# Two orders in the attention loop: a projection piece one group earlier on TensorE, and the copies of finished sums one group up on VectorE

## The chip, the cores and the metric

The kernel runs on one core of one Trainium2 chip. The metric is the device time of one execution in microseconds (us). Of three runs of the kernel before, the median is 2519.34 us (2516.67 to 2519.8). The engines are TensorE (PE, and PEld for its weight loads), VectorE (DVE), ScalarE (ACT), GpSimd (POOL) and SyncE (SP). Each engine takes its instructions strictly in the order in which the program lists them.

## The reference

Eight sequences of 1024 tokens with 512 features pass a causal attention of 16 heads (32 features each), a residual and a layer norm, then a layer of eight experts of which each token takes the best one, a residual and a layer norm. All is float32.

```python
Q, K, V = x @ W_Q.T, x @ W_K.T, x @ W_V.T           # split in 16 heads
attn  = einsum('bhqd,bhkd->bhqk', Q, K) * scale      # causal mask
y     = einsum('bhqk,bhkd->bhqd', softmax(attn), V)
x     = layernorm(x + y @ W_O.T)
probs = softmax(x @ router_w.T + router_b)
x     = layernorm(x + (x @ expert_w[top1].T + expert_b[top1]) * max(probs))
```

## The kernel before

`attend` handles the eight sequences (batches) one after the other. A batch has four units (`u` = 0 to 3) of four heads. The work of a unit is a chain through the engines:

- **projections**: Q and K of a unit are four tiles `("p", u, i)` of 12 matmuls each (L975), made in three pieces of four matmuls, two units ahead. ScalarE rounds the finished tile to its high part (`high`, L646) and VectorE subtracts it to get the low part (`low`, L750). Only then is the PSUM bank free (`proj_free`), and the next tile's first piece can start in it. DMAs of SP and POOL (L443) put the parts into the stacks.
- **maxima**: before a unit's scores are exponentiated, the row maxima of all its scores are needed. 38 maximum tiles (L1032) are computed one unit ahead and reduced on VectorE (`reduce_tile`, L789 or, with the causal mask, L794). Three PSUM banks take turns (`max_ring`), so maximum tile i waits until VectorE has reduced tile i-3.
- **scores**: 12 groups (`j` = 0 to 11, called first to twelfth here) of four tiles (L1044), each followed by an Exp on ScalarE (L704). Two banks take turns in units 0 and 1, more in units 2 and 3.
- **weighing**: two groups later (`LAG` = 2) `weigh` (L1064) multiplies the probabilities with V into `y_ps` and with ones into `den_ps`, 8 instructions of four column tiles. A unit's sums run over groups 1 to 4 (first half of the queries) and 5 to 12 (second half). At the end of a half VectorE copies `y_ps` (`copy_y`, L819) and transposes `den_ps` (`turn_sums`, L827), and only then may the first `weigh` of the next half overwrite them. `divide` (L832 to L838) comes later.

The order inside a group is written out. TensorE does, for h = 0 to 3, the maximum tiles due, score tile h, and at h = 0 and h = 2 one projection piece each if the group has pieces. Behind score tile 1 comes `weigh` of the group two back. A group has four or five maximum tiles due: one ahead of score 0, one ahead of score 1, the rest ahead of scores 2 and 3. So exactly two lie ahead of `weigh`. ScalarE does the four Exps, and `high` behind the second Exp of the group in which a tile is completed. VectorE's list for a group is: copies if due; the first two maximum tiles; `divide` of an old half if due; `low` if a tile was completed; the other maximum tiles.

The function `pieces` gives each group its projection pieces. In unit 0 there are nine pieces (3 to 11) for eight groups, so one group has two. Pieces 5, 8 and 11 complete tiles, in the third, sixth and eighth group. In unit 1 the tiles are completed in the second, fourth, sixth and eighth group. The last `weigh` of the half before stands in the second group (for the second half of the unit before) and in the sixth (for the first half of this unit).

The first copy of a batch, in unit 0, also waits for `scattered`: GpSimd's indirect DMAs (L563, in groups 1 to 4) send the rows of the batch before from `rows`, which this copy overwrites.

After the eight batches, `run_experts` takes the last part of the span; the change does not touch it.

Of the kernel before, what the change touches and what calls it, by code (L numbers as in the profile page):

```python
# [45 lines left out]
LAG = PROBS - 1  # L46
# [102 lines left out]
def attend(nc, region_end, xt, xt_raw, x_t, x_rows, router_w_t, router_b, w_qk_parts, w_vo, dispatched):  # L149

    with ExitStack() as ctx:
# [79 lines left out]
        HALF0 = BANK // P  # L231
# [139 lines left out]
        def max_bank(u, i):  # L371

            return max_ring(u)[i % len(max_ring(u))]
# [26 lines left out]
        def pieces(u, j):  # L400

            if j >= 8:
                return ()
            return range((3 * j + 1) // 2, (3 * (j + 1) + 1) // 2) if u else range(3 + 9 * j // 8, 3 + 9 * (j + 1) // 8)

        def opening_maxima(j):

# [2 lines left out]
        def tiles_made(u, j):  # L410

            return [p // 3 for p in pieces(u, j) if p % 3 == 2]

        def maxima(u, j):

            begin, end = MAX_GROUPS[u > 0]
            if not begin <= j < end or u + 1 == UNITS:
                return []
            return list(range(MTILES * (j - begin) // (end - begin), MTILES * (j + 1 - begin) // (end - begin)))
# [324 lines left out]
        def _(dve):  # L744
            def low(b, u, i):

                bank, _ = place_of(b, ("p", u, i))
                n = 4 * tile_turn(b, u) + i
                dve.wait_ge(part_high.sem, part_high.early(n + 1) if b is None else part_high.at(b, n + 1))
                nc.vector.tensor_tensor(parts[:, i % 2, LO, :], place[bank][:, :], parts[:, i % 2, HI, :].bitcast(F32),  # L750
                                        ALU.subtract).then_inc(proj_free[bank].sem, 1)
# [31 lines left out]
            def one_pass(b, last):  # L783
                def reduce_tile(u, i):
                    qb, heads, j, cols, diag = MAX_TILES[i]
                    bank = max_bank(u, i)
                    dve.wait_ge(max_full.sem, max_full.at(b, MTILES * u + i + 1))
                    if diag is None:
                        nc.vector.tensor_reduce(tile_max[:, j, heads[0]:heads[0] + 1, qb], bank[:, 0:cols], AX.X, ALU.max)\  # L789
                            .then_inc(max_free.sem, 1)  # L790
                        return
                    for place, h in enumerate(heads):
                        tile = bank[:, place * cols:(place + 1) * cols]
                        top = nc.vector.tensor_tensor_reduce(  # L794
                            out=tile, in0=tile, in1=mask_qk[:, BANK - cols:BANK], scale=1.0, scalar=-3.0e38, op0=ALU.add,
                            op1=ALU.max, accum_out=tile_max[:, j, h:h + 1, qb])
                    top.then_inc(max_free.sem, 1)

                def unit_max(u):

                    half = BANK // P
                    dve.wait_ge(max_free.sem, max_free.at(b, MTILES * (u + 1)))
                    if u:
                        wait_job(dve, b, proj_full, ("m", u - 1))
                    rm = row_max[:, :].rearrange("p (h t) -> p h t", h=4)
                    nc.vector.tensor_copy(rm[:, :, 0:half], tile_max[:, 0, :, 0:half]).then_inc(max_step.sem, 1)
                    nc.vector.tensor_tensor(rm[:, :, half:ROWT], tile_max[:, 0, :, half:ROWT],
                                            tile_max[:, 1, :, half:ROWT], ALU.max).then_inc(max_ready.sem, 1)
# [5 lines left out]
                def copy_y(n):  # L814

                    weighed(dve, b, GROUPS * (n // HALVES) + (HALF0 if n % HALVES == 0 else GROUPS))
                    if n == 0:
                        dve.wait_ge(scattered.sem, scattered.at(b, 0))
                    nc.vector.tensor_copy(y_of(n), y_ps[:, :].rearrange("p (t q) -> p t q", q=P))\  # L819
                        .then_inc(y_copied.sem, 1)  # L820
# [3 lines left out]
                def turn_sums(n):  # L824

                    dve.wait_ge(y_ready.sem, y_ready.at(b, n))
                    nc.vector.transpose(sums[:, :], den_ps[:, :]).then_inc(sums_copied.sem, 1)  # L827

                def divide(n):

                    dve.wait_ge(sums_copied.sem, sums_copied.at(b, n + 1))
                    nc.vector.reciprocal(inv[:, :], squares(sums[:, :])[:, :, 0]).then_inc(recip_done.sem, 1)  # L832
                    dve.wait_ge(recip_done.sem, recip_done.at(b, 2 * n + 1))
                    nc.vector.transpose(squares(sums[:, :]), inv[:, :].unsqueeze(2).to_broadcast([P, BANK // DH, DH]))\
                        .then_inc(recip_done.sem, 1)
                    dve.wait_ge(recip_done.sem, recip_done.at(b, 2 * n + 2))
                    dve.wait_ge(y_copied.sem, y_copied.at(b, n + 1))
                    nc.vector.tensor_tensor(y_of(n), y_of(n), sums[:, :].rearrange("p (t q) -> p t q", q=P), ALU.mult)\  # L838
                        .then_inc(y_ready.sem, 1)

                def residual(tb):

                    bank = wait_job(dve, b, proj_full, ("o", tb))
                    dve.wait_ge(x_in_dma[tb % 2].sem, x_in_dma[tb % 2].at(b, 16 * (tb // 2 + 1)))
                    nc.vector.tensor_tensor(rows[:, tb, 0:D], bank[:, :], x_in[:, tb % 2, :], ALU.add)\
                        .then_inc(proj_free[place_of(b, ("o", tb))[0]].sem, 1)
                    wait_job(dve, b, proj_free, ("o", tb))
                    nc.vector.bn_stats(stats[:, tb, :], rows[:, tb, 0:D]).then_inc(norm_step.sem, 1)
                    dve.wait_ge(norm_step.sem, norm_step.at(b, 2 * tb + 1))
                    nc.vector.bn_aggr(mv[:, tb, :], stats[:, tb, :]).then_inc(norm_step.sem, 1)  # L850
# [20 lines left out]
                    destinations(b - 1)  # L871
                for u in range(UNITS):
                    for j in range(GROUPS):
                        if u and j == LAG:
                            copy_y(2 * u - 1)
                            turn_sums(2 * u - 1)
                        if j == HALF0 + LAG:
                            copy_y(2 * u)
                            turn_sums(2 * u)
                            if u == UNITS - 1:  # L880
                                divide(2 * u)
                        due = maxima(u, j)
                        for i in due[0:2]:
                            reduce_tile(u + 1, i)
                        if u and j == LAG + 1:
                            divide(2 * u - 1)
                        if u + 2 < UNITS:
                            for i in tiles_made(u, j):
                                low(b, u + 2, i)
                        for i in due[2:]:  # L890
                            reduce_tile(u + 1, i)
                        if u + 1 < UNITS:
                            if j == MAX_GROUPS[u > 0][1] - 1:
                                unit_max(u + 1)
                        if u < UNITS - 1 and j == HALF0 + LAG + 1:
                            divide(2 * u)
                        if u == UNITS - 1 and j in O_GROUP:
                            residual(O_GROUP[j])
# [48 lines left out]
            for b in range(BATCHES):  # L947
                one_pass(b, b == BATCHES - 1)
# [625 lines left out]
```

## Time and profile before

| what | value |
|---|---|
| median of three runs | 2519.34 us (2516.67 to 2519.8) |
| the profiled execution | 2532.87 us, of which span 2531.0 us |
| mean granted TensorE clock | 0.978 |
| busy, share of the span | PE 92%, DVE 58%, ACT 41%, POOL 34% |
| the first copies of a batch (L819), batches 1 to 8 | at 135.52, 401.11, 666.38, 933.13, 1203.20, 1468.01, 1734.52, 2003.23 us |

Times in the timeline count from the start of the span. A row of the timeline has the start, the duration, the engine, the line, the output and inputs, the count of merged instructions, and in brackets how long the engine (or the weight loader) had been idle before it and whose work ended that. The time of a row of several instructions is that from the first start to the last end; matmuls overlap, so the next matmul can start before the end of the one ahead. The examples are from the fourth batch (from 905 us). The other batches repeat its pattern to some hundredths of a microsecond, except where the granted clock differs.

### The profile page before, as it was taken

Reading aid. Unit: us, or ns where it says so; the run is one execution under the profiler, and the core shown is the slowest. Engines: PE = TensorE matmul, PEld = TensorE weight load, DVE = VectorE, ACT = ScalarE, POOL = GpSimd, SP = SyncE. Lnnn points to the kernel's source line nnn. Section 1 sums busy time; section 2 is a strip of 40 time slices with the busy share of each in tenths; the row PEclk is TensorE's granted clock in tenths of the full one; section 3 lists DMA queues with packets and bytes.
Section 4 is the critical chain, followed back from the end, with each engine's and each line's share of the span. In section 5 each row is a group of like instructions: output and inputs, shape, how many; then the busy total and the mean of one; then the engine's idle time right before and its main releaser. Section 6 shows DMA issues by size and latency. Waiting matters only on the chain. (4 is left out here: it accounts for less than half of the span.)

```text
span 2531.0 us, 41857 instructions
## 1 busy us (share of the span) xinstructions
PE 2318.8 (92%) x14080; PEld 1481.0 (59%) x14081; DVE 1459.2 (58%) x3931; ACT 1028.7 (41%) x2105; POOL 872.9 (34%) x1535
## 2 busy tenths in 40 slices
PE   1999999999999999999999999999999999619998
PEld 1754675557554755476546755575547554418886
DVE  2566366736564566537664667366735665356665
ACT  2245424552446234632454245424452345133333
POOL 2323323332323242333232332323332422225665
PEclk9999999999999999999999999999999999759999
DMA  8632254314531353225321633144313520164443
GB/s 294 164 80 84 67 134 126 109 60 110 149 101 68 84 169 82 93 71 172 80 92 52 172 91 101 64 120 135 109 64 89 158 76 22 55 201 146 151 143 120
DMA packets 130935, 282.07 MB, mean 111 GB/s; under 512 B 33026, under 2 KB 42242, under 8 KB 128452
## 3 DMA queue, kind: packets, MB, share of 16 engines
q1 hardware_dynamic: 100920, 208.62, 27.9%
q0 software_dynamic: 28304, 70.64, 9.3%
q8 instruction: 104, 1.70, 0.3%
q10 hardware_dynamic: 1536, 0.53, 0.1%
q14 instruction: 71, 0.58, 0.1%
HBM read 133.04 MB, written 47.53 MB: 71 GB/s over the span
## 5 line engine op out<-in xcount | busy, mean ns | idle before, releaser
L704 ACT ACTIVATE probs<-score 128x512 f32<-128x512 f32 (+3 forms) x1216 | 561.4, 493 | 548.5 <-PE score L1044 522.2
L579 POOL TENSOR_SCALAR_AFFINE_SELECT probs<-probs 128x256 f32<-128x256 f32 x512 | 215.2, 424 | 729.6 <-ACT probs L704 726.5
L794 DVE CUSTOM_DVE_ANT_0 maxp<-maxp,mask_qk 128x384 f32<-128x384 f32 (+3 forms) x696 | 323.5, 506 | 220.4 <-PE maxp L1032 205.4
L1044 PE MATMUL score<-q_stack,k_stack 97*128 97x512 f32 (+2 forms) x1216 | 426.7, 374 | 24.2 <-ACT probs L704 21.8
L975 PE MATMUL proj<-xt,w_qk 128*128 128x512 f32 x1284 | 361.8, 398 | 53.7 <-DMA w_qk<-w_qk_parts 53.0
L1032 PE MATMUL maxp<-k_stack,q_stack 96*128 96x512 f32 (+2 forms) x1024 | 329.7, 366 | 28.0 <-DVE tile_max L789 15.7
L1064 PE MATMUL y_ps<-probs,v 128*32 128x512 f32 (+3 forms) x3072 | 329.8, 501 | 12.3 <-DVE rows L819 12.1
L1064 PE MATMUL den_ps<-probs,ones_f 128*32 128x512 f32 (+3 forms) x3072 | 322.3, 490 | 0.0
L1044 PEld LDWEIGHTS score<-q_stack,k_stack 97*128 97x128 f32 x1216 | 224.8, 189 | 143.6 <-ACT probs L704 96.7
L975 PEld LDWEIGHTS proj<-xt,w_qk 128*128 128x128 f32 x1284 | 237.9, 190 | 108.9 <-DMA w_qk<-w_qk_parts 50.5
L1032 PEld LDWEIGHTS maxp<-k_stack,q_stack 96*128 96x128 f32 x1024 | 181.0, 189 | 156.2 <-DVE tile_max L794 52.2
L789 DVE TENSOR_REDUCE tile_max<-maxp 128x1 f32<-128x512 f32 x328 | 219.2, 682 | 45.6 <-PE maxp L1032 44.5
L1519 PE MATMUL ye_ps<-weight,xt_tile 128*128 x864 | 214.8, 398 | 0.0
L443 POOL DMA_DIRECT2D k_stack<-parts x256 | 125.7, 498 | 209.8 <-DVE parts L750 188.2
L988 PE MATMUL proj<-q_stack,xt 128*128 128x512 f32 x684 | 189.1, 399 | 0.6 <-DMA rb<-router_b 0.6
L443 POOL DMA_DIRECT2D q_stack<-parts x256 | 127.7, 506 | 179.4 <-DVE parts L750 176.2
L1064 PEld LDWEIGHTS den_ps<-probs,ones_f 128*32 128x32 f32 x3072 | 100.0, 110 | 151.8 <-issue 124.1
L1519 PEld LDWEIGHTS ye_ps<-weight,xt_tile 128*128 128x128 f32 x864 | 164.2, 190 | 36.2
L586 POOL TENSOR_TENSOR parts<-rows,parts 128x512 fp32r<-128x512 f32 x64 | 75.6, 1187 | 214.7 <-ACT parts L678 214.7
L750 DVE TENSOR_TENSOR parts<-proj,parts 128x512 fp32r<-128x512 f32 x107 | 73.7, 688 | 125.9 <-ACT parts L646 124.9
L1087 PE MATMUL proj<-q_stack,parts 128*128 128x512 f32 x576 | 142.5, 396 | 2.3 <-POOL parts L586 2.3
L794 DVE DVE_READ_ACCUMULATOR2_ANT tile_max<- 128x1 f32 x1024 | 144.2, 141 | 0.0
(163 smaller groups left out, 2991.6 us busy)
## 6 DMA issues: line engine op xcount, KB each, us to landing
w_qk<-w_qk_parts SPq DMA_DIRECT2D x64, 512.0 KB
q_stack<-w_vo_parts SPq DMA_DIRECT2D x16, 2048.0 KB, 8.1
q_stack<-parts SPq DMA_DIRECT2D x512, 64.0 KB
k_stack<-parts SPq DMA_DIRECT2D x512, 64.0 KB
got<-dispatched SPq DMA_DIRECT2D x75, 257.0 KB, 2.6
xt_raw<-x_t SPq DMA_DIRECT2D x32, 512.0 KB, 9.3
q_stack<-parts POOLq DMA_DIRECT2D x256, 64.0 KB, 2.3
k_stack<-parts POOLq DMA_DIRECT2D x256, 64.0 KB, 2.4
```

The source lines that it names most:

```text
L443: eng.dma_start(dst[DH * block_row:DH * (block_row + 1), h, t * BANK:(t + 1) * BANK].bitcast(F32), parts[DH * h:DH * (h + 1), t, part, :]. ...
L579: nc.gpsimd.affine_select(out=block, in_=block, compare_op=ALU.is_ge, fill=0.0, base=0, pattern=[[0, 2], [1, P]], channel_multiplier=-1)\
L704: nc.scalar.activation(probs[:, 4 * (n % PROBS) + h, c:BANK], score_bank(u, 4 * j + h)[:, c:BANK], ACT.Exp, scale=SCALE).then_inc(exp_done ...
L789: nc.vector.tensor_reduce(tile_max[:, j, heads[0]:heads[0] + 1, qb], bank[:, 0:cols], AX.X, ALU.max)\
L794: top = nc.vector.tensor_tensor_reduce(out=tile, in0=tile, in1=mask_qk[:, BANK - cols:BANK], scale=1.0, scalar=-3.0e38, op0=ALU.add, op1=A ...
L975: mm = nc.tensor.matmul(place[bank][:, :], w_qk[:, o, ws, k, :], xt[:, xs, k, t * BANK:(t + 1) * BANK], start=c == 0, stop=c == 3 * KT - 1)
L988: mm = nc.tensor.matmul(place[bank][:, :], xt[:, xs, k, tb * P:(tb + 1) * P], wv[:, ws, k, :], start=c == 0, stop=c == 3 * KT - 1)
L1032: mm = nc.tensor.matmul(bank[:, place * cols:to], q_st[u % SETS][0:3 * DH, h, qb * P:(qb + 1) * P], k_st[u % SETS][0:3 * DH, h, j * BANK:j ...
L1044: nc.tensor.matmul(score_bank(u, i)[:, c0:BANK], k_st[u % SETS][0:3 * DH + 1, h, kb * P:(kb + 1) * P], q_st[u % SETS][0:3 * DH + 1, h, t * ...
L1064: mm = nc.tensor.matmul((den_ps if sums_too else y_ps)[DH * h:DH * (h + 1), c:BANK], ones_f[:, :] if sums_too else v[:, kb, head * DH:(hea ...
L1087: mm = nc.tensor.matmul(bank[:, :], parts[:, tb % 2, ys, g * P:(g + 1) * P], wo[:, ws, g, :], start=c == 0, stop=c == 3 * UNITS - 1)
L1519: mm = nc.tensor.matmul(y_ps[s][:, :], xt[:, s % 2, xs, k * P:(k + 1) * P], weight[:, ws, bass.ds(e * (KT * D) + k * D, D)], start=False, ...
```

## The change

In unit 0, the group with two projection pieces becomes the seventh in place of the eighth: piece 10 moves into the third slot of the seventh group, and piece 11, which completes the tile, moves in the eighth group from behind score 2 to behind score 0. On VectorE the copy and the transpose move from the top of the third and seventh group to the second and sixth, behind that group's first two maximum tiles, ahead of `low` and the other maximum tiles. In unit 3 there are no maximum tiles and no `low`, so nothing that VectorE does stands between the old place and the new.

```diff
-            return range((3 * j + 1) // 2, (3 * (j + 1) + 1) // 2) if u else range(3 + 9 * j // 8, 3 + 9 * (j + 1) // 8)
+            return range((3 * j + 1) // 2, (3 * (j + 1) + 1) // 2) if u else range(3 + (9 * j + 1) // 8, 3 + (9 * j + 10) // 8)
...
                 for u in range(UNITS):
                     for j in range(GROUPS):
-                        if u and j == LAG:
+                        due = maxima(u, j)
+                        for i in due[0:2]:
+                            reduce_tile(u + 1, i)
+                        if u and j == LAG - 1:
                             copy_y(2 * u - 1)
                             turn_sums(2 * u - 1)
-                        if j == HALF0 + LAG:
+                        if j == HALF0 + LAG - 1:
                             copy_y(2 * u)
                             turn_sums(2 * u)
                             if u == UNITS - 1:
                                 divide(2 * u)
-                        due = maxima(u, j)
-                        for i in due[0:2]:
-                            reduce_tile(u + 1, i)
                         if u and j == LAG + 1:
                             divide(2 * u - 1)
```

TensorE, unit 0, from the third slot of the seventh group to the weighing of the eighth. Before:

```order
L1032 MATMUL proj<-k_stack,q_stack 128x512
L1044 MATMUL score<-q_stack,k_stack 128x512
L975 MATMUL proj<-xt,w_qk 128x512 x4
L1032 MATMUL maxp<-k_stack,q_stack 128x512
L1044 MATMUL score<-q_stack,k_stack 128x512
L1064 MATMUL y_ps<-probs,v 32x512 x4
L1064 MATMUL den_ps<-probs,ones_f 32x512 x4
L1032 MATMUL maxp<-k_stack,q_stack 128x512
L1044 MATMUL score<-q_stack,k_stack 128x512
L975 MATMUL proj<-xt,w_qk 128x512 x4
```

And now:

```order
L975 MATMUL proj<-xt,w_qk 128x512 x4
L1032 MATMUL maxp<-k_stack,q_stack 128x512
L1044 MATMUL score<-q_stack,k_stack 128x512
L1032 MATMUL proj<-k_stack,q_stack 128x512
L1044 MATMUL score<-q_stack,k_stack 128x512
L975 MATMUL proj<-xt,w_qk 128x512 x4
L1032 MATMUL maxp<-k_stack,q_stack 128x512
L1044 MATMUL score<-q_stack,k_stack 128x512
L1064 MATMUL y_ps<-probs,v 32x512 x4
L1064 MATMUL den_ps<-probs,ones_f 32x512 x4
```

The last piece of the tile stood behind the weighing and the third score; now it stands ahead of the second score, and one piece more is in the seventh group.

VectorE, unit 0, the sixth group and the top of the seventh. L750 is `low`, L789 a maximum tile. Before:

```order
L750 TENSOR_TENSOR parts<-proj,parts 128x512
L789 TENSOR_REDUCE tile_max<-maxp 128x1
L789 TENSOR_REDUCE tile_max<-proj 128x1
L789 TENSOR_REDUCE tile_max<-maxp 128x1
L819 COPY rows<-y_ps 128x4x128
L827 STREAM_TRANSPOSE sums<-den_ps 128x512
L789 TENSOR_REDUCE tile_max<-maxp 128x1
```

And now:

```order
L819 COPY rows<-y_ps 128x4x128
L827 STREAM_TRANSPOSE sums<-den_ps 128x512
L750 TENSOR_TENSOR parts<-proj,parts 128x512
L789 TENSOR_REDUCE tile_max<-maxp 128x1
L789 TENSOR_REDUCE tile_max<-proj 128x1
L789 TENSOR_REDUCE tile_max<-maxp 128x1 x2
```

The copy and the transpose have passed `low` and three maximum tiles.

VectorE, unit 1, the second group and the top of the third. L794 is a masked maximum tile, of two rows. Before:

```order
L750 TENSOR_TENSOR parts<-proj,parts 128x512
L794 ISA maxp,tile_max<-maxp,mask_qk 128x384
L794 ISA tile_max 128x1
L794 ISA maxp,tile_max<-maxp,mask_qk 128x512
L794 ISA tile_max 128x1
L819 COPY rows<-y_ps 128x4x128
L827 STREAM_TRANSPOSE sums<-den_ps 128x512
```

And now:

```order
L819 COPY rows<-y_ps 128x4x128
L827 STREAM_TRANSPOSE sums<-den_ps 128x512
L750 TENSOR_TENSOR parts<-proj,parts 128x512
L794 ISA maxp,tile_max<-maxp,mask_qk 128x384
L794 ISA tile_max 128x1
L794 ISA maxp,tile_max<-maxp,mask_qk 128x512
L794 ISA tile_max 128x1
```

Here they have passed `low` and two maximum tiles. The lists of ScalarE, GpSimd and SyncE are the same as before.

## Rows read from the trace of the kernel before

**Rows 1.** The page, busy time of each engine.
```profile
PE 2318.8 (92%) x14080; PEld 1481.0 (59%) x14081; DVE 1459.2 (58%) x3931; ACT 1028.7 (41%) x2105; POOL 872.9 (34%) x1535
```
**Rows 2.** Timeline, fourth batch, unit 0, eighth group (columns told above).
```profile
941.65 1.09 PE L975 MATMUL proj<-xt,w_qk 128*128 128x512 f32 x4
...
942.78 0.60 ACT L646 ACTIVATE parts<-proj 128x512 fp32r<-128x512 f32 x1 [2.85 <-PE proj L975]
942.93 0.40 PE L1044 MATMUL score<-q_stack,k_stack 97*128 97x512 f32 x1
...
943.41 0.69 DVE L750 TENSOR_TENSOR parts<-proj,parts 128x512 fp32r<-128x512 f32 x1 [3.63 <-ACT parts L646]
...
944.75 0.19 PEld L1032 LDWEIGHTS maxp<-k_stack,q_stack 96*128 96x128 f32 x1 [1.80 <-DVE tile_max L789]
```
**Rows 3.** Windows: stretch, us, PE busy, granted clock, DMA share, GB/s.
```profile
411.10:420.10 9.00, 7.58 (x47) 1.00 0.36 77
...
943.10:952.10 9.00, 7.58 (x34) 0.81 0.40 112
```
**Rows 4.** Timeline, second batch, the first two copies.
```profile
401.11 0.68 DVE L819 COPY rows<-y_ps 128x512 f32<-128x512 f32 x1
...
437.47 0.69 DVE L819 COPY rows<-y_ps 128x512 f32<-128x512 f32 x1
```
**Rows 5.** Timeline, fourth batch, unit 0, sixth and seventh group.
```profile
929.74 0.40 PE L1064 MATMUL den_ps<-probs,ones_f 128*32 128x128 f32 x8
...
930.28 0.14 DVE L794 DVE_READ_ACCUMULATOR2_ANT tile_max<- 128x1 f32 x1
...
932.07 0.19 PEld L1032 LDWEIGHTS maxp<-k_stack,q_stack 96*128 96x128 f32 x1 [0.99 <-DVE tile_max L789]
...
933.13 0.68 DVE L819 COPY rows<-y_ps 128x512 f32<-128x512 f32 x1
...
934.35 0.65 DVE L789 TENSOR_REDUCE tile_max<-maxp 128x1 f32<-128x512 f32 x1
```
**Rows 6.** Timeline, fourth batch, unit 1, second and third group.
```profile
969.79 0.40 PE L1064 MATMUL den_ps<-probs,ones_f 128*32 128x128 f32 x8
...
970.66 0.69 DVE L750 TENSOR_TENSOR parts<-proj,parts 128x512 fp32r<-128x512 f32 x1 [0.56 <-ACT parts L646]
...
971.54 1.09 PE L975 MATMUL proj<-xt,w_qk 128*128 128x512 f32 x4
...
972.39 0.69 DVE L819 COPY rows<-y_ps 128x512 f32<-128x512 f32 x1
...
973.23 1.07 PE L1064 MATMUL y_ps<-probs,v 128*32 128x512 f32 x8 [0.24 <-DVE rows L819]
```
**Rows 7.** Timeline, fourth batch, unit 1, sixth and seventh group.
```profile
988.59 0.40 PE L1064 MATMUL den_ps<-probs,ones_f 128*32 128x128 f32 x8
...
990.68 1.09 PE L975 MATMUL proj<-xt,w_qk 128*128 128x512 f32 x4
...
992.21 1.07 PE L1064 MATMUL y_ps<-probs,v 128*32 128x512 f32 x8
```
**Rows 8.** Timeline, fourth batch, unit 2, second and third group.
```profile
1020.14 0.14 DVE L794 DVE_READ_ACCUMULATOR2_ANT tile_max<- 128x1 f32 x1
...
1021.20 0.39 PE L1032 MATMUL maxp<-k_stack,q_stack 96*128 96x512 f32 x1
...
1022.37 1.07 PE L1064 MATMUL y_ps<-probs,v 128*32 128x512 f32 x8 [0.66 <-DVE rows L819]
```
**Rows 9.** Timeline, fourth batch, unit 2, sixth and seventh group.
```profile
1035.04 0.68 DVE L789 TENSOR_REDUCE tile_max<-proj 128x1 f32<-128x512 f32 x1
...
1035.84 0.37 PE L1032 MATMUL proj<-k_stack,q_stack 96*128 96x384 f32 x1
...
1037.06 1.06 PE L1064 MATMUL y_ps<-probs,v 128*32 128x512 f32 x8 [0.62 <-DVE rows L819]
```
**Rows 10.** Windows (us, clock, DMA share, GB/s), seventh batch, ahead of its first copy.
```profile
1731.02:1731.52 0.50, 1.00 0.17 58
```

## The prediction, written before the run

> **What bounds the kernel now.** I read the page first: TensorE is busy for 92% of the span, the next engine, VectorE, for 58% [rows 1]. A gain or a loss therefore has to be a wait on TensorE that goes, comes or changes its length; work taken off another engine is worth nothing by itself, and the change takes none off. I then went through the timeline of the fourth batch around the six places per batch that the change touches, and noted where TensorE's stream stands still and what released it. The reader is to see three kinds of stop: one long one in the eighth group of unit 0 [rows 2], one before the weighing that starts a new half, which waits for the copy [rows 6, 8, 9], and one before a maximum tile or a projection piece, which waits for a bank that VectorE has not given back yet [rows 5]. Last I looked at the granted clock, since TensorE alternates between 2.4 and 1.2 GHz.
>
> **Part A, the pieces (gain).** Before, the piece that completes the tile starts at 941.65. ScalarE stands 2.85 us before it can convert it (942.78), VectorE stands 3.63 us in front of `low` (943.41), and the three maximum tiles behind `low` wait too, though two were there. So TensorE's next maximum tile finds its bank full: its score starts at 942.93 and occupies it for 0.21 us (512 columns at 2.4 GHz), the next weights load at 944.75, after 1.80 us of idle loader, and the matmul goes 0.11 us later [rows 2]: a gap of 944.86 - 943.14 = 1.7 us. With the piece ahead of the second score, `high` follows the second Exp and `low` ends before the third maximum tile is there. The four matmuls are not saved, only moved from the eighth to the seventh group, where neither the loader nor VectorE is full, so they count zero. What is late next is the reduction of the third maximum tile itself: TensorE still waits about 0.2 us for it, and on the other side a wait for an Exp in the same stretch (0.2 us) is filled by the moved piece. A gives 1.7 us per batch, 13.6 us in eight.
>
> **Part B, the copy in unit 0.** The copy and the transpose together hold VectorE for 934.35 - 933.13 = 1.22 us [rows 5]. Their new start, S, is the later of two events: the end of the weighing plus 0.07, and the start of the accumulator read of the second maximum tile, since the next instruction starts with it. The weighing ends at 930.14, so S = 930.28. (The short spacings that I add, 0.07, 0.11, 0.17, 0.19, 0.60, 0.64 us, are my readings of how close such instructions follow each other in the same timeline; each is good to 0.05.) Then come 1.22 for copy and transpose, 0.60 for `low` and 0.68 for the third maximum tile: its bank is free at 932.78 in place of 932.02 (0.05 ahead of the load at 932.07) [rows 5]. The first maximum tile of the seventh group needs exactly that bank, three back in the ring. TensorE was already waiting 0.99 us there, and waits 0.76 more. Nothing comes back at the weighing, because TensorE did not wait for the copy in this place. Cost 0.8 us per batch.
>
> **Parts C to F, the other four copies.** The same reckoning, always with two effects: the wait for the copy goes, and something else that stood ahead of the copy is now behind it.
> C, unit 1, second group: the weighing ends at 970.19, S = 970.26, and `low` starts at 971.48 in place of 970.66, so 0.82 later. The next projection piece starts at 971.54, 0.19 after the old end of `low`: it was waiting for just this bank, and moves by 0.82. The weighing loses its 0.24 us of waiting for the copy [rows 6]. Cost 0.82 - 0.24 = 0.6 us.
> D, unit 1, sixth group: the weighing ends at 988.99, S = 989.06, `low` runs from 990.28 to 990.97, and with 0.19 the next piece starts at 991.16 in place of 990.68. Ahead of the weighing at 992.21 there was a wait of 0.1 [rows 7]. Cost 0.4 us.
> E, unit 2, second group: S = 1020.14. 1.22 for the copies, 0.64 for the third maximum tile and 0.17 to the matmul: the second maximum tile of the third group starts at 1022.17 in place of 1021.20, 0.97 later, and the weighing gets 0.66 back [rows 8]. Cost 0.3 us.
> F, unit 2, sixth group: the third maximum tile, now at 1035.04 [rows 9], comes 1.22 later; its end is 1036.94 and the second maximum tile of the seventh group starts 0.17 behind that, at 1037.11 in place of 1035.84. The weighing gets back 0.62. Cost 0.65 us.
> In unit 3 there is nothing between the old place and the new: zero. All of C to F is 1.95 us per batch. These delays persist, since behind each place the releasing engine is waiting for TensorE too (VectorE is idle before its next maximum tile), so both move together.
> The bounds for the copies, from both sides: at best nothing is lost and the waits of 0.24, 0.66 and 0.62 plus the 0.1 all go, a gain of 1.6 us per batch; at worst nothing comes back and C to F cost 0.82 + 0.5 + 0.97 + 1.27 = 3.6, with B 4.4 us. I take the sum worked out, 0.8 + 1.95 = 2.75 per batch, 22.0 us in eight, since each of its terms goes by rows in the place itself.
>
> **The clock.** In four of the eight batches the gap of part A is followed by a stretch at 1.2 GHz: a window of 9 us has a mean clock of 0.81 (fourth batch) where another has 1.00 (second batch) [rows 3]; four windows of eight read the one, four the other. From the first to the second copy of the batch it is 437.47 - 401.11 = 36.36 us at full clock [rows 4], and 972.39 - 933.13 = 39.26 in the fourth batch [rows 5, 6]. Over the four disturbed batches the same difference sums up to 8.6 us. Without the gap these should go. Whether they do in the plain runs, I can't see: their median is 13.5 us below the profiled execution, and fewer drops would be one reason. The account for the drops lies between 0 and 8.6 us of gain, and below zero if the new waits draw drops of their own. The wait in B becomes one of about 1.6 us (0.82 of standing matmul stream plus 0.76), nearly the 1.7 that drew them. I take the middle, 4.3 us of gain.
> The Trainium skill, "TensorE: Matmul & The Clock Gate", section "A second HAM failure mode: psum-queue depth-cycling", says that frequent small idles between groups of matmuls, as bank cycling makes them, are enough to let the clock swing between its two levels. The trace agrees in that a gap of 1.7 us goes before each of these four drops; it does not show the same after the shorter ones. By this rule the five lengthened waits are candidates, which is the first rival below.
>
> **The sum.** Against the profiled execution's own time of 2532.87: -13.6 + 22.0 = +8.4 us for the waits, -4.3 for the clock, +4.1 us in all, 2536.9. The plain runs lie lower by 13.5, so I set the same difference on their median: 2519.34 + 4.1 = 2523.4 us. A measurement of this kernel can tell about 0.2%, some 5 us, from no change.
>
> **Rivals.**
> 1. Slower: the drops move from the old gap to the new one in the seventh group of unit 0. The price is 8.6 us for four batches at the new place; if those of the old place are gained, the sum is +8.4, 2527.7 us; if the plain runs had none before, it is +17, 2536. It decides from the point at which more than one of eight batches drops there. For it: the new gap is as long as the old. Against it: behind it four projection matmuls follow at once, and stops of this size at the start of unit 1 (the wait for the maxima's DMA) draw no drop in any batch.
> 2. Faster: the copies cost half of what I reckon, because a release that I put down to `low` or to a maximum tile comes earlier than the rows suggest. Then -13.6 + 11 - 4.3 = -7, 2512 us; with the best bound of the copies (-12.5 us for them) and all drops gone it would be -13.6 - 12.5 - 8.6 = -35, 2485 us, for which every wait on a bank would have to have slack that rows 5 to 9 deny.
> 3. The first copy of a batch now waits for the scatter DMAs of the batch before. Its old place left 2.85 us more. In the seventh batch the engines still moved 58 GB/s until 1731.5 [rows 10], with S at 1734.52 - 2.85 = 1731.67. A completion that comes 0.5 us late would delay `low` and three maximum tiles by as much: up to +4 us over eight batches, 2527 us. Against it: the traffic ends ahead of S in all batches.
> 4. The piece moves without effect, because ScalarE's `high` or `low` is late for another reason: A is worth nothing, +22, 2541 us. Against it: the 2.85 and 3.63 us in rows 2 name the chain.
>
> **How the numbers follow.** The forecast with its own range of 2519 to 2528 gets 0.45, rival 1 0.20, rival 2 0.23, rival 3 0.08, rival 4 0.04. The range for 8 in 10 is 2510 to 2533. Faster by over 0.2% (below 2514.3): most of rival 2, 0.19. Slower (above 2524.4): rivals 1, 3 and 4 and a good third of the forecast, 0.43. Within: 0.38.
>
> **What would show it.** In the changed profile: A holds if the wait of `high` in the eighth group is gone and the loader's 1.80 us shrinks to a few tenths. B holds if the load of the first maximum tile of the seventh group waits some 1.7 us instead of 0.99. C and D hold if the projection pieces of the third and seventh group of unit 1 start 0.8 and 0.5 us later, counted from the end of the weighing ahead, and wait for `low`. E and F hold if the wait for the copy disappears there and one of about a microsecond for a maximum tile's bank takes its place. From the first copy's weighing to the last of unit 2, a batch without drops should be about 1.1 us longer. I am wrong if the waits on banks stay as they are while the waits for the copy go, or if windows at half clock appear where there were none.

## The result and the profile after

The changed kernel takes 2526.7 us (median of 12 runs, 2522.41 to 2539.88); the kernel before 2519.07 us on the same chip (12 runs). The ratio is 1.0038, 95% interval 1.0021 to 1.0055: slower, by some 9.6 us with an interval of 5.3 to 13.9 us. 2523.4 us was forecast, with 2510 to 2533 as the range. One of the five executions of the last kernel under The experiments took 3261.09 us at a mean granted clock of 0.655, in place of 0.979 to 0.982 in the other four; its ratio leaves that one out.

The span of the changed kernel's profiled execution (2522.1 us) is shorter than that of before (2531.0 us), against the ratio. So whole spans are not compared here. I compare stretches of a batch, and take each from the batches in which neither the granted clock nor a DMA disturbs it. Their marks are the starts of the short weighings that end a half (`den_ps`, 128x128, eight per batch). The first stretch runs from the sixth group of unit 0 to the second group of unit 1, and so on to the second group of unit 3:

| undisturbed stretch, us | first (A and B) | second (C) | third (D) | fourth (E) | fifth (F) | sum |
|---|---|---|---|---|---|---|
| before | 37.13 | 18.80 | 31.00 | 14.41 | 25.54 | 126.88 |
| after | 36.19 | 19.26 | 31.32 | 14.60 | 26.06 | 127.43 |
| difference | -0.94 | +0.46 | +0.32 | +0.19 | +0.52 | +0.55 |

The last four repeat in all eight batches to 0.03 us. The two stretches behind the fifth, where the change has nothing to do, are 8.72 and 27.24 us in both. The first is disturbed in four batches of before and in six of after. Summed over the batches as they were, disturbances included, the five stretches take 1023.7 us before and 1031.6 us after: +7.9 us, close to what the medians differ by (7.6 us). Of it, 8 x 0.55 = 4.4 us are waits in the order itself; the other 3.5 us are disturbances of the first stretch. That plain runs have as many disturbances is assumed. Outside the five stretches the profiled execution of before is 16.8 us longer; 11.2 of these lie between the last weighing of a batch and the first of the next, where the change does nothing.

The timeline of the changed kernel, fourth batch, unit 0, sixth and seventh group, answers to [rows 5]:

```profile
930.16 0.40 PE L1064 MATMUL den_ps<-probs,ones_f 128*32 128x128 f32 x8
...
930.70 0.69 DVE L819 COPY rows<-y_ps 128x512 f32<-128x512 f32 x1
...
931.93 0.65 DVE L750 TENSOR_TENSOR parts<-proj,parts 128x512 fp32r<-128x512 f32 x1
932.50 0.67 DVE L789 TENSOR_REDUCE tile_max<-maxp 128x1 f32<-128x512 f32 x1
...
933.23 0.19 PEld L1032 LDWEIGHTS maxp<-k_stack,q_stack 96*128 96x128 f32 x1 [1.74 <-DVE tile_max L789]
```

The loader's wait has grown from 0.99 to 1.74 us. The copy starts right behind the second maximum tile, and the reduction whose bank TensorE needs comes fourth in the row. In the eighth group, to be read against [rows 2]:

```profile
941.68 0.59 ACT L646 ACTIVATE parts<-proj 128x512 fp32r<-128x512 f32 x1
...
942.30 0.69 DVE L750 TENSOR_TENSOR parts<-proj,parts 128x512 fp32r<-128x512 f32 x1 [0.66 <-ACT parts L646]
...
944.22 0.19 PEld L1032 LDWEIGHTS maxp<-k_stack,q_stack 96*128 96x128 f32 x1 [0.34 <-DVE tile_max L789]
```

ScalarE no longer waits for the piece, VectorE 0.66 us in place of 3.63, and the gap of 1.7 us is down to a loader wait of 0.34 us. In units 1 and 2 TensorE now waits for a bank; in three of the four places this takes the place of the wait for the copy [rows 6, 8, 9], and in the sixth group of unit 1 (988.03) there was none for the copy [rows 7]:

```profile
968.77 1.20 PE L975 MATMUL proj<-xt,w_qk 128*128 128x512 f32 x4 [0.50 <-DVE parts L750]
...
988.03 1.20 PE L975 MATMUL proj<-xt,w_qk 128*128 128x512 f32 x4 [0.16 <-DVE parts L750]
...
1019.38 0.50 PE L1032 MATMUL maxp<-k_stack,q_stack 96*128 96x512 f32 x1 [0.66 <-DVE tile_max L794]
...
1034.54 0.44 PE L1032 MATMUL proj<-k_stack,q_stack 96*128 96x384 f32 x1 [0.98 <-DVE tile_max L789]
```

The clock, windows of 9 us from 2 us behind the first weighing of a batch, so right behind the lengthened wait (columns as in [rows 3]):

```profile
132.70:141.70 9.00, 7.93 (x46) 1.00 0.36 87
397.50:406.50 9.00, 7.90 (x37) 0.81 0.37 87
663.50:672.50 9.00, 6.87 (x26) 0.62 0.37 88
932.20:941.20 9.00, 7.97 (x46) 1.00 0.37 87
1196.80:1205.80 9.00, 7.49 (x41) 1.00 0.37 88
1461.40:1470.40 9.00, 7.55 (x35) 0.81 0.38 90
1727.00:1736.00 9.00, 6.78 (x32) 0.81 0.38 89
1995.10:2004.10 9.00, 7.91 (x37) 0.81 0.38 89
```

In five of eight batches a part of this window runs at 1.2 GHz, in the third batch twice as long. Before, no batch had this at this place. The place behind the old gap is clean. Ahead of the five the loader had waited 1.74 us in two batches (the second and the eighth) and, with the copy's wait below added, 2.11 to 2.85 us in three; in the three batches without half clock it was 1.74, 1.74 and 2.21 us. The first copy waits for the scatters in four batches, longest in these two:

```profile
663.09 0.69 DVE L819 COPY rows<-y_ps 128x512 f32<-128x512 f32 x1 [0.89 <-DMA dispatched<-rows,dest]
...
1726.68 0.69 DVE L819 COPY rows<-y_ps 128x512 f32<-128x512 f32 x1 [0.96 <-DMA dispatched<-rows,dest]
```

### The profile page after: what moved, and what is told of

Read it like the earlier page. It is cut to its first block and busy times, and to the rows that moved or that the text cites. A ratio compares the mean times of both kernels' runs of the same rounds, so it can differ in the third digit from the quotient of the medians.

```text
span 2522.1 us, 41857 instructions
## 1 busy us (share of the span) xinstructions
PE 2318.3 (92%) x14080; PEld 1480.3 (59%) x14081; DVE 1460.0 (58%) x3931; ACT 1032.4 (41%) x2105; POOL 875.4 (35%) x1535
## 5 line engine op out<-in xcount | busy, mean ns | idle before, releaser
L794 DVE CUSTOM_DVE_ANT_0 maxp<-maxp,mask_qk 128x384 f32<-128x384 f32 (+3 forms) x696 | 323.2, 505 | 242.1 <-PE maxp L1032 241.1
L789 DVE TENSOR_REDUCE tile_max<-maxp 128x1 f32<-128x512 f32 x328 | 217.8, 684 | 47.4 <-PE maxp L1032 46.5
L794 DVE DVE_READ_ACCUMULATOR2_ANT tile_max<- 128x1 f32 x1024 | 144.2, 141 | 0.0
L988 PEld LDWEIGHTS proj<-q_stack,xt 128*128 128x128 f32 x684 | 124.2, 189 | 28.1 <-issue 5.9
```

The source lines that it names most:

```text
L794: top = nc.vector.tensor_tensor_reduce(out=tile, in0=tile, in1=mask_qk[:, BANK - cols:BANK], scale=1.0, scalar=-3.0e38, op0=ALU.add, op1=A ...
L988: mm = nc.tensor.matmul(place[bank][:, :], xt[:, xs, k, tb * P:(tb + 1) * P], wv[:, ws, k, :], start=c == 0, stop=c == 3 * KT - 1)
```

## The experiments

The theory to test: every copy moved up costs a wait on a bank, the pieces by themselves save 1.7 us per batch, and the half-clock stretches follow the longest gap. The rivals: only the clock counts; or VectorE's total work counts, so that any wait taken away comes back. The undisturbed stretches (first: at full clock, without waits for a DMA):

| kernel | first | second | third | fourth | fifth | half-clock batches in the first stretch | ratio to before, 95% interval |
|---|---|---|---|---|---|---|---|
| before | 37.13 | 18.80 | 31.00 | 14.41 | 25.54 | 4 | 1 |
| changed | 36.19 | 19.26 | 31.32 | 14.60 | 26.06 | 5 | 1.0038 [1.0021, 1.0055] |
| pieces only | 35.45 | 18.80 | 31.00 | 14.41 | 25.54 | 1 | 0.9925 [0.9903, 0.9946] |
| copies only | 37.90 | 19.26 | 31.33 | 14.60 | 26.06 | 5 | 1.0091 [1.0073, 1.0109] |
| first copy old | 35.45 | 19.25 | 31.33 | 14.60 | 26.06 | 0 | 0.9977 [0.9964, 0.9991] |
| behind the third tile | 35.83 | 18.50 | 30.88 | 13.77 | 24.95 | 0 | 0.9873 [0.9854, 0.9892] |
| `low` first | 36.64 | 19.27 | 31.50 | 14.60 | 26.07 | 4 | 1.0045 [1.0028, 1.0062] |
| scatters earlier | 36.19 | 19.25 | 31.32 | 14.60 | 26.06 | 0, but 6 ahead of it | 1.0094 [1.0073, 1.0115] |
| behind the third, first copy old | 35.44 | 18.47 | 30.88 | 13.76 | 24.96 | 0 | 0.9865 [0.9844, 0.9885] |

**Pieces only.** The line of `pieces` changed as in the change, nothing else.

> Only the projection pieces are moved; all copies stay where they were. I look at five stretches of each batch, bounded by the weighings that end a half (128-column den_ps rows): before they last 37.13, 18.80, 31.00, 14.41 and 25.54 us at full clock, in the changed kernel 36.19, 19.26, 31.32, 14.60 and 26.06. Bank theory (every copy moved up costs a wait on a bank, the pieces alone save 1.7 us per batch): the first stretch is 35.4 to 35.5, the other four as before, and with the gap gone no half-clock stretch stands in the first stretch. Ratio to before 0.991 to 0.995. Clock theory (the slowdown of the changed kernel comes only from half-clock stretches that moved, not from waits on banks): the first stretch is 36.2 as in the changed kernel, ratio 0.994 to 0.998.

Measured: 2500.27 us against 2517.98, first stretch 35.45, the others as before. 37.13 - 35.45 = 1.68 us is the gap of part A. The clock theory's 36.2 is refuted. One half-clock stretch is left, in the fifth batch, not at the place of the gap but at the start of unit 1, behind a loader wait of 1.62 us for the maxima's DMA; the prediction had said, from the profile of before, that these stops draw none.

**Copies only.** The change without the line of `pieces`.

> Only the copies are moved up; the pieces stay where they were. Bank theory: first stretch 37.13 + 0.8 = 37.9 at full clock, the other four as in the changed kernel (19.26, 31.32, 14.60, 26.06), so 2.3 us per batch, 18 us, plus half-clock stretches at either gap: ratio 1.007 to 1.012. Clock theory: first stretch 37.1, the total moves only by drops, ratio 1.000 to 1.004.

Measured: 2542.32 us, first stretch 37.90 (+0.77), the others to 0.03 as in the changed kernel. The two parts of the change add up: -1.68 + 0.77 = -0.91, and the changed kernel has -0.94.

**First copy old.**

```diff
+                        if u == 0 and j == HALF0 + LAG:
+                            copy_y(0)
+                            turn_sums(0)
                         for i in due[0:2]:
                             reduce_tile(u + 1, i)
...
-                        if j == HALF0 + LAG - 1:
+                        if u and j == HALF0 + LAG - 1:
```

> As the changed kernel, but the first copy of a batch (unit 0) is back at the top of the seventh group; pieces new, the other copies up. Bank theory: first stretch 35.4, the other four as in the changed kernel; no half-clock stretch behind the sixth group and no wait of the first copy for the scatter DMAs (in the changed kernel 0.2 to 1.0 us in four batches). Against before -1.7 + 1.5 = -0.2 us per batch and 8.7 us of drops less: ratio 0.995 to 0.999, so 0.4 to 0.7% faster than the changed kernel. If the slowdown came from the four later copies rather than from the first, the ratio stays near that of the changed kernel, 1.003.

Measured: 2513.59 us, ratio 0.9977, so 0.6% below that of the changed kernel. All eight windows behind the weighing read a clock of 1.00, and no copy waits for a DMA. Two of them, where the changed kernel had 0.81 and 0.62:

```profile
397.00:406.00 9.00, 8.71 (x50) 1.00 0.37 87
660.70:669.70 9.00, 8.64 (x50) 1.00 0.38 88
```

One copy, moved back by one group, takes away 0.74 us of waiting per batch and all half-clock stretches of this place. In this pair the half clock goes with the wait. In all profiles together, no batch of the kernels with a loader wait of 0.99 us here has a half-clock stretch at this place, and 14 of the 32 batches of the four kernels with 1.74 us or more have one. The wait is not enough by itself: "scatters earlier", below, has 1.74 to 1.75 us in all eight batches and none.

**Behind the third tile.** The copies stand in the same groups as in the change, but later in the group: the third maximum tile, `low` and the `divide` of an old half are now all ahead of them (the lines that move `low` and `divide` are left out here):

```diff
+                        for i in due[2:3]:
+                            reduce_tile(u + 1, i)
                         if u and j == LAG - 1:
                             copy_y(2 * u - 1)
                             turn_sums(2 * u - 1)
...
-                        for i in due[2:]:
+                        for i in due[3:]:
                             reduce_tile(u + 1, i)
```

> Pieces new; all copies of units 0 to 2 stand in the second and sixth group behind `low` and the third maximum tile, one tile (in unit 0 two tiles) ahead of their old place. Bank theory: the bank that the next but one maximum tile ahead of the weighing needs and the projection bank are both given back before the copy starts, and the copy ends one tile earlier than before. The first stretch is 35.4, the second 18.80 - 0.24 = 18.55, the third 30.9, the fourth 14.41 - 0.6 = 13.8, the fifth 25.54 - 0.6 = 24.95: 3.2 us per batch, 26 us, and 8.7 us of drops: ratio 0.986 to 0.991. Rival (VectorE's total work is what counts behind these places, so a wait that goes comes back at the next maximum tile): as with the pieces alone, 0.991 to 0.995.

Measured: 2488.79 us, 1.27% below before. Four of five stretches hit the forecast to 0.05 us; the first is 0.4 longer. The rival falls: the waits that go do not come back. At the place of [rows 9], the sixth group of unit 2, this kernel's timeline (its line 1066 is `weigh`) reads:

```profile
1016.62 0.68 DVE L819 COPY rows<-y_ps 128x512 f32<-128x512 f32 x1
...
1017.45 1.06 PE L1066 MATMUL y_ps<-probs,v 128*32 128x512 f32 x8
```

The matmul of the weighing has no wait any more, where it had 0.62 us.

**`low` first.** As the change, with `low` moved ahead of the copies.

> As the changed kernel, but in VectorE's list `low` stands ahead of the copy (order: two maximum tiles, low, copy and transpose, the other maximum tiles). The places without `low` (unit 2) are as in the changed kernel: fourth and fifth stretch 14.60 and 26.06 us. Where `low` stands (units 0 and 1) there are two theories. Ring theory: the projection bank is given back in time, but now the third maximum tile comes still later (copy and transpose follow `low`), and the ring of three banks stops TensorE one or two steps on: first stretch 36.6 (changed 36.19), second 19.3 (19.26), third 31.5 (31.32), ratio to before 1.003 to 1.008. Projection bank theory: the cost in unit 1 was that of the projection bank alone, so the second stretch goes back to 18.6 and the third to 30.9, ratio 0.999 to 1.002.

Measured: 36.64, 19.27, 31.50, ratio 1.0045: the ring theory to 0.05 us. Giving back the projection bank in time gains nothing as long as the third maximum tile is behind the copy. Two banks are waited for one after the other, and the copy has to be behind both.

**Scatters earlier.**

```diff
-        SCATTER_AT = {0: (0, 1), 1: (2, 3), 2: (4, 5), 3: (6, 7)}
+        SCATTER_AT = {0: (0, 1, 2), 1: (3, 4, 5), 2: (6, 7)}
```

> As the changed kernel, but GpSimd issues the eight scatters of the batch before in the first three groups of unit 0 (3, 3, 2) in place of the first four (2 each). In the changed kernel the first copy waits for them in four of eight batches (0.2 to 1.0 us). If that wait matters, it is gone here and up to 3 us of the whole come back: ratio to before 1.001 to 1.003. Against it stands that GpSimd also masks the probabilities of these groups, so that three scatters in a row delay a mask by 1 us and TensorE's weighing behind it: then the stretches behind are unchanged, but the time ahead of the first weighing that I count (101.2 us from the last of the batch before) gets longer, and the ratio is 1.004 or more.

Measured: ratio 1.0094. The copy's wait for the DMAs is gone and the five stretches are as in the changed kernel, but the time from the last weighing of a batch to the first of the next is 103.6 to 106.8 us, where "`low` first", run on the same chip beside it, has 101.2 to 104.0. The waits of TensorE, in total, times and longest, first here and then in the changed kernel:

```profile
PE score L1044 <- ACT probs L704: 33.7, 68, 3.5
```

```profile
PE score L1044 <- ACT probs L704: 19.9, 64, 0.5
```

The second theory's numbers hold, but its mechanism, from the mask over the weighing, isn't shown. The long wait, ahead of the second batch:

```profile
386.50 0.42 POOL L579 TENSOR_SCALAR_AFFINE_SELECT probs<-probs 128x256 f32<-128x256 f32 x1
387.56 0.43 DVE L794 CUSTOM_DVE_ANT_0 proj<-proj,mask_qk 128x256 f32<-128x256 f32 x1 [4.29 <-remote]
387.60 0.66 ACT L704 ACTIVATE probs<-score 128x256 f32<-128x256 f32 x2 [5.05 <-remote]
...
388.04 0.39 PE L1044 MATMUL score<-q_stack,k_stack 97*128 97x256 f32 x1 [3.52 <-ACT probs L704]
```

The mask is late, right behind three scatters, but ScalarE and VectorE stand as well, each in front of work that needs no mask, and the profile names nothing of this core that released them ("remote"). Ahead of the eighth batch they go on before the mask starts. This happens ahead of five batches, and no other kernel here has such a wait over 1.5 us; what releases them stays open. A half-clock stretch stands at or right behind each of the five waits, and one more ahead of the fourth batch. Two of the six are of double length. If each costs 1.65 us per single length, as in the first stretch, they are 8 x 1.65 = 13 us (an estimate) of the 21.3 us by which this kernel is longer than "`low` first" between its batches.

**Behind the third, first copy old.** As "behind the third tile", with the first copy of the batch at its old place.

> As the kernel with the copies behind the third maximum tile, but the first copy of the batch (unit 0) is at its old place, the top of the seventh group. There the first stretch took 35.84 us where the pieces alone give 35.45. If the first copy makes the difference (unit 0 has two maximum tiles behind the third, of which the first is needed by the ring ahead of the weighing), the first stretch is 35.45 and the others stay 18.50, 30.88, 13.77 and 24.95: 0.4 us per batch better, ratio 0.984 to 0.988. If not, 35.84 and ratio 0.985 to 0.989.

Measured: 2494.68 us against 2530.07 in this group of runs, ratio 0.9865. The first stretch is 35.44: in unit 0, where two tiles lie behind the third, the first of them is needed ahead of the weighing too, and the old place was the right one. The answer on the copies of this kernel has no waiter left:

```profile
L819 DVE COPY rows<-y_ps x64: 679/688/695, 134.5 to 2128.3; 128x512 f32<-128x512 f32 x64
...
who waited for it (us, times):
```

Its ratio is the lowest found; that of "behind the third tile" (0.9873) lies inside its interval.

**Before again.** The unchanged kernel, profiled once more.

> The kernel before itself, profiled once more. Its five stretches at full clock should be 37.13, 18.80, 31.00, 14.41 and 25.54 again to 0.05 us, if these are a property of the order and not of the execution. The half-clock stretches behind the gap of the eighth group of unit 0 (four of eight batches in the first profile) should come again in some of the eight, not the same ones, if they depend on where in time the gap falls. Time 2511 to 2530.

Measured: 37.15, 18.80, 30.99, 14.41, 25.56, in 2530.93 us. Again four of eight batches have the half-clock stretch behind the eighth group, but not the same ones:

```profile
409.90:418.90 9.00, 7.58 (x33) 0.81 0.33 82
...
942.90:951.90 9.00, 7.58 (x49) 1.00 0.39 101
```

The second batch was clean in the first profile and is not here; the fourth the other way round [rows 3]. The kernel before had a median of 2517.98 us beside the first four kernels and of 2530.07 us beside these, on another chip. The stretches are the same on both: the last four of the pieces kernel, on the first chip, and of this one differ by 0.02 us at most. The time between the last weighing of a batch and the first of the next is 100.7 to 102.9 us in the pieces kernel on the one, and 102.2 to 105.9 us here. That could explain how the profiled span of before lies above that of a slower kernel, if they were taken on two such chips: it is 101.2 to 104.4 us in the profile of before and 100.4 to 102.0 in that of the changed kernel. Which chip either was taken on is not on record.

## Why the prediction was right, and where it was off

- **Part A** was right: 1.7 us forecast, 1.68 measured with the pieces alone. The link from the piece over `high` and `low` to the full ring was the cause, as said.
- **Part B** was right: 0.8 forecast, 0.74 to 0.77 measured (changed kernel less "first copy old"; copies only less before). The loader wait of "some 1.7 us" is 1.74.
- **Parts C to F** had the right sign, mechanism and order, and each was oversized by 0.1: forecast 0.6, 0.4, 0.3, 0.65, measured 0.46, 0.32, 0.19, 0.52, in sum 1.49 in place of 1.95. I had added full durations and spacings one after the other. Counted from the weighing ahead, the four waiting matmuls start 0.14 to 0.16 us earlier than forecast, all alike. An instruction that is already queued behind the other runs shorter: `low` takes 0.65 us behind the transpose (931.93) where it took 0.69 after a wait [rows 6]. That is part of it; the rest, in the short spacings that I had read to 0.05 each, I did not separate. Waits in the order were thus forecast as +8.4 us and came out as +4.4.
- **The clock term** failed in its sign. "I take the middle, 4.3 us of gain" supposed that the drops would mostly go. They went from the old gap and came at the new one, six lengths of half clock (the third batch has two) for four: rival 1, whose mechanism and place were named, and to which I gave 0.20. The 8.6 us that I booked as drops were mis-sized, too: each costs some 1.65 us in the stretch, 6.6 in four batches; the rest, 2.1 us, was the wait for the maxima's DMA at the start of unit 1, of up to 1.5 us, in two of them. That plain runs have drops as well, which I could not see, is told by their mean granted clock: 0.979 over 17 executions of before, 0.982 over six with the pieces only, 0.981 over twelve with the first copy old, 0.978 over twelve of the changed kernel.
- **Rival 3** happened as well: 0.9, 0.3, 0.2 and 1.0 us of waiting for the scatters in four batches, 2.4 us in all. I had argued from the traffic of before, which had ended ahead of S. In the changed kernel it had not: in its seventh batch S would have been 1726.68 - 0.96 = 1725.72, and the engines moved 140 GB/s in the half microsecond from 1725.5, 41 from 1726.0 and 8 from 1726.5. The last scatter was issued 3.6 us ahead of the weighing there, 4.0 us ahead of it before.
- The total is closer than its terms (+4.1 forecast, +7.6 between the medians), and that is luck: 4.0 us too much in the waits stand against 7.8 us too little in the disturbances, which were booked as a gain of 4.3 and came as a loss of 3.5.
- **Rivals 2 and 4** are refuted by "copies only" (2.27 us per batch, where half of the reckoning is 1.4) and "pieces only" (1.68 us of gain).

## What to carry to other kernels

Before moving an instruction up to cut the wait for it, list what it passes, and ask for each which resource it gives back and who waits for that next: here a copy and a transpose of together 1.2 us passed `low` and reductions that give back the banks of a ring of three, and TensorE lost more on those banks than it had lost on the copy. The best of the places tried is right behind the last release that is needed ahead of the consumer, not as early as the data allow. Two changes in one step should be timed apart: the good one was worth -0.75%, the other +0.9%.

## What was not expected of the hardware

- A matmul stream that stands for 1.3 us (the loader for 1.74 us) can be followed by half clock and need not be. With a loader wait of exactly that length it was in two of four batches of the changed kernel and in none of eight of "scatters earlier"; with the longer gap of before it was in four of eight, in both profiles, but not in the same four. What else decides stays open. No half-clock stretch stands at the four later copies of a batch in any profile; TensorE's matmuls wait up to 1 us there.
- The Trainium skill, "TensorE: Matmul & The Clock Gate", section "A second HAM failure mode: psum-queue depth-cycling", told that small idles from bank cycling suffice for half clock, if they are frequent. The pair "changed" and "first copy old" agrees in part: removing 0.74 us from one wait removed all drops behind it. "Scatters earlier" shows the same wait without a drop.
- Two chips ran the same program 12 us apart (2517.98 and 2530.07 us), while stretches that no DMA disturbs were equal to 0.03 us. What differs between the chips, no run here shows.
